# Second half of a step, re-ordered: half of the output projection ahead of the products with the state, two pieces of the second feed-forward product together

## What is computed

```python
x = x + attn(layernorm(x));  x = x + ffn(layernorm(x))

# attn: r, k, v, g are projections (512x512) of x mixed with its predecessor
def step(state, inp):                       # a chunk of Q = 64 tokens
    rc, kc, vc = inp
    att = rc @ kc * w_mat                   # scores
    yc = att @ vc + rc @ state * wb         # products with V, product with the state
    new_state = ws * state + kc * wk @ vc
    return new_state, yc
out = group_norm(y) * gamma + beta ; out = (out * silu(g)) @ Wo.T

# ffn
D = gelu(x16 @ W0.T + bias0) ; E = D @ W1.T + bias1
```

## Time and profile before

| | us |
|---|---|
| median of 3 runs | 2078.05 |
| lowest, highest | 2074.58, 2080.48 |
| the profiled execution | 2075.69 |
| its span, first to last instruction | 2073.9 |
| PE busy in it | 2002.3 (97%) |
| DVE busy | 1738.2 (84%) |
| ACT busy | 1293.5 (62%) |
| POOL busy | 317.5 (15%) |

### The profile page before, as it was taken

The page is one execution under the profiler, slowest core; times in us unless marked ns, Lnnn a source line. Parts: engine busy times, 40 slices in busy tenths (PEclk is TensorE's granted clock), DMA queues, the critical chain, the costliest instruction groups (busy, mean ns, idle before and its releaser), DMA issues.

```text
span 2073.9 us, 64752 instructions
## 1 busy us (share of the span) xinstructions
PE 2002.3 (97%) x27206; PEld 1423.9 (69%) x27206; DVE 1738.2 (84%) x3687; ACT 1293.5 (62%) x2081; POOL 317.5 (15%) x329
## 2 busy tenths in 40 slices
PE   5889999999999999999999999999999999999999
PEld 5777667667666767766766776676776667667666
DVE  7778889888888988888988888898888888888761
ACT  7876565676566666655657765666765656666452
POOL 1111111111111111111111111111111111111110
PEclk8999999999999999999999999999999999999999
DMA  6977677888777788777778877778887877887777
GB/s 214 220 199 237 177 236 216 248 239 233 200 233 220 236 241 241 213 226 227 230 231 245 248 203 225 234 215 247 250 231 202 231 220 230 250 238 203 216 249 250
DMA packets 428979, 471.97 MB, mean 228 GB/s; under 512 B 259600, under 2 KB 309392, under 8 KB 428688
## 3 DMA queue, kind: packets, MB, share of 16 engines
q1 hardware_dynamic: 427056, 467.64, 77.2%
q10 hardware_dynamic: 1632, 0.18, 0.1%
HBM read 316.21 MB, written 25.17 MB: 165 GB/s over the span
## 4 chain that ended last, share of the span: by engine, by line
PE 81%; DMA 4%; SPq 4%; DVE 3%; ACT 3%; issue 3%; POOL 0%; ACTq 0%; DVEq 0%
PE F L1132 20%; PE F L1068 17%; PE B L879 10%; PE B L1040 8%; PE sc L879 7%; PE YT L911 6%; PE YT L879 3%; PE YT L963 2%; DMA y<-ygT 2%; PE sc L941 2%; PE YT L982 2%; DMA ring<-w_dram 1%; SPq L2027 1%; PE YT L1012 1%; PE F L836 1%
## 5 line engine op out<-in xcount | busy, mean ns | idle before, releaser
L1132 PE MATMUL F<-ring,hT 128*128 128x512 f16 x1984 | 467.5, 379 | 0.0
L1068 PE MATMUL F<-xT,ring 128*128 128x256 f16 x3840 | 449.3, 273 | 5.1 <-ACT hT L1768 3.7
L1068 PEld LDWEIGHTS F<-xT,ring 128*128 128x128 f16 x3840 | 369.8, 98 | 64.9 <-issue 8.0
L1132 PEld LDWEIGHTS F<-ring,hT 128*128 128x128 f16 x1984 | 189.1, 98 | 197.9 <-issue 0.5
L879 PE MATMUL B<-mix,WT 128*128 128x256 f16 x2304 | 267.5, 273 | 0.4 <-DVE gT L1372 0.3
L1768 ACT ACTIVATE hT<-F,b,f_rho 128x256 f16<-128x256 f32 x480 | 243.5, 560 | 37.9 <-PE F L1068 37.9
L879 PEld LDWEIGHTS B<-mix,WT 128*128 128x128 f16 x2304 | 222.6, 98 | 33.8 <-DVE gT L1372 0.6
L276 DVE SCALAR_TENSOR_TENSOR mixf<-dx,maa,xnT 128x256 f32<-128x256 f32 x512 | 238.6, 526 | 0.1
L1725 ACT ACTIVATE Shl<-S 128x256 f16<-128x256 f32 x128 | 53.1, 415 | 263.7 <-PE YT L982 148.6
L1971 POOL TENSOR_TENSOR Shl<-S,Shl 128x256 f16<-128x256 f32 x128 | 89.2, 697 | 734.7 <-ACT Shl L1725 734.7
L1719 ACT ACTIVATE att<-att 128x512 f16<-128x512 f32 x256 | 147.5, 624 | 68.3 <-DVE att L1333 68.3
(11 more groups left out here) (196 smaller groups left out, 2997.6 us busy)
## 6 DMA issues: line engine op xcount, KB each, us to landing
ring<-w_dram SPq DMA_DIRECT2D x512, 512.0 KB, 4.6
kx<-kT SPq DMA_DIRECT2D x96, 256.0 KB, 3.8
rx<-rT SPq DMA_DIRECT2D x96, 256.0 KB, 4.4
xa<-in_L_attn_x SPq DMA_DIRECT2D x32, 512.0 KB, 7.6
vbd<-vN SPq DMA_DIRECT2D x256, 64.0 KB, 3.1
x<-in_L_attn_x SPq DMA_DIRECT2D x32, 512.0 KB, 6.1
out<-x SPq DMA_DIRECT2D x31, 512.0 KB, 3.8
w_dram<-ring SPq DMA_DIRECT2D x20, 256.0 KB, 3.8
```

The source lines that it names most:

```text
L1068: mm = eng.matmul(up_place(f, j)[:, i * BT:(i + 1) * BT], ring[:, use % RING, i, a * C + kk * P:a * C + (kk + 1) * P], xT[:, :, kk, :], st ...
L1132: mm = eng.matmul(F[:, t, :], hT[:, k, rows(t)], ring[:, use % RING, i, a * C:(a + 1) * C], start=(k == 0 and a == 0), stop=(k == NH - 1 a ...
```

## The change

No instruction is added or removed. In `pe_step`, `pe_Wo(0)` moves in front of `pe_from_state(0)` and `pe_scores(2)`, and `pe_down(1)` moves up to stand right behind `pe_down(0)`, in front of `pe_kv(1)` and `pe_scores(3)`. `pe_Wo(1)` and `pe_down(2)` then follow the scores directly. In `dve_steady`, `dve_gate(1)` goes in front of both `mix_lo`, which now stand together; `dve_residual(0)` goes in front of `dve_take_y(0)`, `dve_weigh(3)` in front of `dve_state(2)`, and `dve_variance(0)` behind `dve_state(3)`. In `act_steady`, `act_weights_hi(3)` goes in front of `act_state_hi(2)`. The PE part holds for every step, the DVE and ACT parts for steps 3 to 31. The lists of POOL and SP are as before.

```diff
         if ff:
             pe_up(eng, n, 7)
+        if tail:
+            pe_Wo(eng, n, 0)
         if att_n:
             pe_from_state(eng, n, 0)
             pe_scores(eng, n, 2)
             pe_prepare(eng, n, "sc2")
-        if tail:
-            pe_Wo(eng, n, 0)
             pe_prepare(eng, n, "Wo0")
         if ff:
             pe_down(eng, n - 2, 0)
+            pe_down(eng, n - 2, 1)
         if att_n:
             pe_kv(eng, n, 1, n < STEADY)
             pe_scores(eng, n, 3)
...
-        if ff:
-            pe_down(eng, n - 2, 1)
         if tail:
             pe_Wo(eng, n, 1)
...
         dve_state(eng, n, 1)
+        dve_gate(eng, n, 1)
         if ahead:
             mix_lo(eng, n + 1, 0)
-        dve_gate(eng, n, 1)
+            mix_lo(eng, n + 1, 1)
+        dve_residual(eng, n - 1, 0)
         dve_take_y(eng, n, 0)
         dve_weigh(eng, n, 2)
-        if ahead:
-            mix_lo(eng, n + 1, 1)
         dve_weights_lo(eng, n, 2)
-        dve_variance(eng, n, 0)
-        dve_residual(eng, n - 1, 0)
+        dve_weigh(eng, n, 3)
         dve_state(eng, n, 2)
-        dve_weigh(eng, n, 3)
         dve_weights_lo(eng, n, 3)
         dve_state(eng, n, 3)
+        dve_variance(eng, n, 0)
...
         act_square(eng, n, 0)
+        act_weights_hi(eng, n, 3)
         act_state_hi(eng, n, 2)
-        act_weights_hi(eng, n, 3)
```

## The result

The changed kernel takes 2083.35 us (median of 10 runs, 2078.83 to 2086.63), the kernel before beside it 2077.85 (10 runs, 2072.64 to 2080.48). The ratio is 1.0029, with 95% between 1.0017 and 1.0040, which is 6.0 us slower (3.5 to 8.3). The forecast was 2080.0, 2.0 us slower. The profiled execution took 2082.99 us, 7.3 more than the one of before.

A forecast was written before the change was run, and what follows sets the result against it. PE was taken as the bound, with some 24 us open in stalls read as missed instruction packets. -23.2 - 1.9 + 26.1 + 1 = +2.0 us on 2078.05 gave 2080.0 us, range 2068 to 2092.

The forecast's parts named there:

- The bound and the stalls: PE bounds; its stalls in steps 3 to 31 are missed instruction packets: 25.2 us regained, 2 come back, gain 23.2.
- 256 instructions from the start of L982: PE's stretch from the product with the state: 5.2 us after the change, 6.0 before, 6.0 again with the hT wait.
- rival 1: Packets are missed again in L1012 and the second L941; half of 23.6 us comes back, 2090 us; chance 0.14.
- The wait for `hT`: L1132 waits for the later act_gelu(7) in steps 2 to 31: 0.87 us a step, 26.1 us in all.
- near 2055: Time in us if both the stalls are gone and the hT wait in L1132 is absent.
- Products with V of tile 1: DVE's chain ahead of pe_att_v(1) takes 4.46 to 4.56 us against 4.51; cost 1 us, ends 0 and 7.
- the second rival: V products wait: DVE's chain misses by 0.25 us a step, not 0.03; +6.4 us, 2086.4; chance 0.12.
- Step 2: Regains 3.6 us, including 1.5 if the clock fell; pe_Wo(1) waits 1.7 us for the residual; -1.9 us taken.
- Steps 0 and 1 at nothing: Steps 0 and 1 have slack elsewhere or do not contain the moved pair; 0 us.
- The third: The gelu wait is small: 0.4 us a step, 12 us instead of 26, time 2066; chance 0.13.
- fourth: The stalls have nothing to do with packets and stay; 2104.5 us, 2107 for the median; chance 0.05.

The follow-up runs named there:

- e1: The changed kernel with act_gelu(7) ahead of act_state_hi(1) in ACT's list, nothing else; 2088.25 us against 2082.18 of the kernel before, ratio 1.0025.
- e5: The changed kernel with act_gelu(7) ahead of act_state_hi(1) and step 1 in its old order; 2085.46 us against 2084.79 of the kernel before, ratio 1.0020.
- e8: e5 with the last 3 of the 12 matmuls of pe_Wo(0) behind the scores of chunk 2, from step 2 on; ratio 1.0137 to the kernel before.
- e3: The changed kernel with pe_down(1) put back behind pe_scores(3); 2100.34 us against 2082.18 of the kernel before, ratio 1.0085.
- e4: The changed kernel with pe_Wo(0) in its old place in step 1 alone; 2088.30 us against 2082.18 of the kernel before, ratio 1.0029.
- e7: The changed kernel with the old DVE and ACT lists in steps 3 to 31; 2134.36 us against 2079.25 of the kernel before, ratio 1.0265.
- e10: The kernel before with the first 6 of the 12 matmuls of pe_Wo(0) ahead of L982, from step 2 on; 2095.43 us against 2084.79, ratio 1.0061.
- e12: e10 with DVE's mix_lo ahead of take_y and the variance behind the last state; 2078.02 us against 2083.73 of the kernel before, ratio 0.9979.
- e9: The kernel before with the changed kernel's DVE and ACT lists in steps 3 to 31; 2159.44 us against 2079.25, ratio 1.0386.

## Why the prediction was right or wrong, point by point

**The bound and the stalls: right.** PE is the bound on both sides. The forecast was under 5 us on issue and 25.2 us regained less 2 that come back. In the 28 steps the stalls in L982, L941, L1040, L1012 and L1132 went from 24.9 to 4.3 us, 20.6 regained, of which the clock is 1.5 (the 7 slow matmuls near 1860 us). It was 2.6 us less than the 23.2 of the sum. What came back was forecast for L1012 and the scores behind it, and there is nothing there: 1.3 us are in the scores behind L982, 0.6 in L1132, and 2.4 are one stall in the second L982, a place that the prediction did not look at.

One reading in this part was wrong. The "256 instructions from the start of L982" are 128 matmuls with their loads, but the 5.2 and 6.0 us were added up over the blocks up to the end of the second scores, 176 and 180 matmuls. For 128 of them the traces have 5.6 us before, 4.6 in the new order without the wait (e1) and 5.45 with it. So the wait brings the new order to just under the old one and not level with it, and rival 1's condition, "between 5.2 and 6 us", was set against the wrong length.

**The wait for `hT`: right.** 0.87 us a step forecast, 0.83 measured in 26 of 30 steps and less in the other four, 23.7 us in all against 26.1. Its three terms are in the trace: 0.29 to the start of `act_state_hi(1)`, the gelus complete 1.61 us behind the start of the scores, and a lag of under 0.1 us, the shorter of the two that were given. What the prediction weighed too lightly is that stalls come back when this wait goes. It had that in half a sentence ("With the wait of the next paragraph inside it is 6.0 again"), for L1012 and the scores behind it. Its "near 2055" was for a kernel with neither the stalls nor the wait; e1 and e5 show that taking the wait away does not give that kernel but one at 1.0020 to 1.0025.

**Products with V of tile 1: right, on the good side.** The chain of DVE ended in time:

```profile
1022.75 0.48 DVE L1351 SCALAR_TENSOR_TENSOR kv<-YT,flag,headmask 128x256 f32<-128x256 f32 x1
```

That is over at 1023.23, and PE starts L963 at 1023.38. There is 0.15 us from the one to the other, about the lag of the earlier trace rows, and no wait is listed. 0 us for the 1 forecast. In e1, where PE comes 0.8 us earlier, it is 0.25 us a step, the second rival's number, under another condition than it named.

**Step 2: right.** 1.7 us of wait for the residual were forecast. The waits of PE from 200 to 264 us:

```profile
PE B L1040 <- DVE x L1302: 1.6, 1, 1.6
```

From L963 of step 2 to that of step 3 it is 63.11 us against 63.84, 0.7 less, where -1.9 + 0.87 = -1.0 was forecast. The fallen clock that it put into this step on an "if" is in the trace before: 7 matmuls of L1040 from 209.50 us on at a pitch of 0.427.

**Steps 0 and 1 at nothing: wrong, by 2.6 us.** This is the term that failed: "Steps 0, 1 and from 32 on have slack elsewhere or do not contain the moved pair; 0". Step 1 contains `pe_Wo(0)` without any feed-forward part, and there it was the only thing between two pieces of `pe_prepare` that use the same two banks. Taken away, ACT's copy is waited for 2.6 us longer, and nothing later gives it back: the next large wait of PE (L1068, at 183.17 us before and 189.11 after) is 1.11 and 1.14 us. The moved line of the diff stood next to `pe_prepare`, so it could have been read from the order alone. From step 32 on the zero holds, 90.80 us against 90.88.

**The sum.** Forecast +2.0: -23.2 - 1.9 + 26.1 + 1. With what was measured: from step 2 to step 31 it is +1.4, in step 1 +2.6, together +4.0; the ratio says +6.0, with 3.5 and 8.3 as ends, which holds 4.0. That the time came out near is in part luck: 2.0 was the small difference of two terms near 25, and their misses, 2.6 us too much gain on one side and 2.4 + 1 too much cost on the other, nearly cancel. The rest of the 7.3 between the two profiled executions is the 3.3 of start-up that come and go between runs.

**The rivals.** The first (packets missed again) did not happen in the changed kernel. In e1 and e5, without the wait, packets were missed again, but mostly in the second L982 and not in L1012 and L941 as it says. The second did not come: no wait of L963 is listed. The third and fourth are excluded by the 29 waits and the 3.2 us.

## What to carry to other kernels

A wait in an engine that is the bound is worth its length only if nothing else comes in its place. Here DVE's chain was late by 0.25 us a step as soon as it went, and missing packets and other stalls took 15.2 us: taking it away in e1 shortened the typical step by 0.55 us and changed the time by nothing. Ask of every wait that you mean to remove what is late next, in each of the other streams, the one of instructions among them. And follow a moved block through the steps at the start of the pipeline, where most of the work that covers it elsewhere is absent.

## What the runs showed of the hardware that was not expected

PE stalls where many short matmuls follow each other, at places set by the count of instructions: 24 matmuls more moved a break by 24 matmuls. Each of the 43 stalls of over 0.4 us that were followed up (15 before, 28 in after, e1, e5 and e8) ended 1.1 to 1.6 us behind the end of a transfer of 16.4 KB over the instruction queue.

Of the kernels that were run, stalls were few (10 to 15 us in 28 steps) only in those four where PE waited 0.7 us in nearly every step for `hT`, behind the first two matmuls of L1132 (after, e3, e4, e7). A wait of 0.7 us at another place, ahead of the products with V of tile 1 (e8), did not help the stretch behind it: 9.2 us in three stalls. Spreading the long matmuls by 1.3 us (e10) made the longest stall 1.4 us instead of 2.5, but in e12 it was 1.9 again and the total hardly moved.

The lower clock level came behind single idle times of 1.6 to 3.1 us, but not behind all of them: in e1 behind 1.64 and 2.54 us and not behind 2.60, in e5 behind 2.18 and not behind 3.07. In e9 it came in 14 steps behind two waits, of 1.35 and of 0.35 to 0.6 us, with 0.6 us of work between them.

The stalls in the second L982 of a step are not explained (one in after, three each in e1, e5 and e8; 1.6 to 3.4 us idle). They came though the 126 matmuls ahead of them had run for 5.3 to 6.7 us up to the break, where it was 3.1 to 5.5 us ahead of the stalls of the kernel before. Their transfers began only 4.7 to 7.9 us after the start of that stretch, against 1.9 to 4.6 us there. What makes a transfer begin late, no run shows.
